# Narrow-head attentions of a two-layer decoder: the ones-times-maximum products put ahead of the transposed scores in their PSUM accumulation

## The chip, the cores and the metric

The kernel runs on one core of a Trainium2 chip. The metric is the device time of one execution in microseconds (us); before the change it is 4456.8 us, the median of three runs (4455.21 to 4457.26).

## The reference, cut to what matters

Two decoder layers over 16 sequences of 256 tokens, width 256. Three of the four attentions have 16 heads of 16 and are touched by the change: `L0_attn` (causal), `L0_xattn` (keys masked), `L1_attn` (causal, rotary positions). `L1_xattn` (heads of 64) and the two expert blocks are other code.

```python
# _L0_attn_ref / _L1_attn_ref (causal); q, k, v: [16, 16 heads, 256, 16]
s = einsum('bhqd,bhkd->bhqk', q, k) / sqrt(16); s = where(causal, s, -inf)
p = exp(s - max(s, -1)); y = einsum('bhqk,bhkd->bhqd', p, v) / sum(p)
# _L0_xattn_ref: the same without the triangle
scores = where(mask == 0, -1e9, einsum('bhqd,bhkd->bhqk', Q, K) / sqrt(16))
ctx = einsum('bhqk,bhkd->bhqd', softmax(scores), V)
```

## The kernel before, in words

`narrow_attention_phase` runs each of the three attentions as a software pipeline over the 16 sequences; one pass of the loop is a *step*. In a step TensorE (PE) does eight *groups* (`pair_of_heads`, g = 0 to 7), and behind each group two *uses* of the two bank buffers `a_ps[0]` and `a_ps[1]` (`use_bank`): M1, Y1 behind group 0; Q2B, K2B; V1, Z; Q1, K1 (behind group 3); YT0, YT1 (behind 4); YT, Q2A (behind 5); M0, OUT (behind 6); K2A, Y0 (behind 7). The uses are the projections (L1480), transposes (L1470, L1487, L1505), the transposed maxima (L1492) and the product with the values (L1500). All engines' orders are written out by hand; semaphores tie them together.

A group handles two heads of the next sequence and two of the present one:

- *s-heads*: scores with queries on partitions (L1384, `s_ps`). VectorE (DVE) takes their row maxima, negated (L1193/L1194 causal, L1196 otherwise), when `s_full` is raised.
- *t-heads*: the same scores with keys on partitions (L1388, `t_ps`), and on top of them the negated maximum of each query, added by a product of ones with `mT`, three bfloat16 pieces of the maximum (L1401 and L1402 causal, L1406 otherwise). ScalarE (ACT) takes the exponential of the sum (L1303) when `t_full` is raised.

A head of 16 is padded to 32 partitions (`lane`), so a score product uses 32 of the array's 128 rows. The four heads of a group lie in four different lanes: two lanes hold the s-heads, the other two the t-heads.
All waits of a group (for free score banks `s_taken`, `t_taken`, and for the copies of the projections and maxima) stand ahead of its first product. What DVE and ACT do between the groups matters for three uses: Q1 waits for the rounding of Z (ACT L1315, DVE L1245), YT for the division (DVE `divide`: L1254, L1257, which stands behind the maxima of group 4), and M0 for the rounding of YT. In `L1_attn`, POOL turns queries and keys (`rope`, L1100 to L1103) between Q1 and K2A.

Of the kernel before, what the change touches and what calls it, by code (L numbers as in the profile page):

```python
# [30 lines left out]
P = 128  # L31
B, S, D = 16, 256, 256
H = 16
TT = S // P
# [823 lines left out]
def narrow_attention_phase(nc, c, x_res, ident, ins, x_rest):  # L858

    n = c.name  # L860
    GROUPS, PAD = 4, 32
    ONE, DROP = c.dk, c.dk + 1
    with ExitStack() as ctx:
# [10 lines left out]
        s_ps, t_ps, a_ps = bank[0:3], bank[3:6], bank[6:8]  # L874
# [9 lines left out]
        ones3 = sb("ones3", [P, P], BF16)  # L884
# [40 lines left out]
        qT = [sb(f"qT{i}", [P, GROUPS, S]) for i in range(2)]  # L925
        kT = [sb(f"kT{i}", [P, GROUPS, S]) for i in range(2)]
# [5 lines left out]
        mT = sb("mT", [P, GROUPS, S], BF16)  # L932
# [15 lines left out]
        t_full = sem("t_full")  # L948
# [27 lines left out]
        SLOT = [0, 1, 2] * 5 + [1]  # L976
# [45 lines left out]
        with nc.Block() as block:  # L1022
# [330 lines left out]
            def _(pe):  # L1353
                def pair_of_heads(b, u, g):

                    s_of, t_of = (2 * g, 2 * g + 1) if exists(b + 1) else (), t_heads(g) if exists(b) else ()
                    if not s_of and not t_of:
                        return
                    if s_of:
                        if g == 0:  # L1360
                            pe.wait_ge(a_free[Q2A % 2], emptied(b - 1, Q2A))
                            pe.wait_ge(a_free[K2A % 2], emptied(b - 1, K2A))
                        if g == 4:
                            pe.wait_ge(a_free[Q2B % 2], emptied(b, Q2B))
                            pe.wait_ge(a_free[K2B % 2], emptied(b, K2B))
                        pe.wait_ge(s_taken, slots_free(b + 1, g))
                    if t_of:
                        if g == 0:
                            pe.wait_ge(a_free[M0 % 2], emptied(b - 1, M0))
                        if g == 4:  # L1370
                            pe.wait_ge(a_free[M1 % 2], emptied(b, M1))
                        pe.wait_ge(t_taken, slots_free(b, g))
                    pe.sem_inc(tick, 1)

                    def lane(h):
                        return slice(PAD * (h % 4), PAD * (h % 4) + PAD)

                    def tile(h, x, t):
                        return x[lane(h), h // 4, t * P:(t + 1) * P]

                    def score(h, t):
                        keys = (t + 1) * P if c.causal else S
                        to = t * (P if c.causal else S)
                        return pe.matmul(s_ps[SLOT[h]][:, to:to + keys], tile(h, qT[1 - u], t), kT[1 - u][lane(h), h // 4, 0:keys], start=t == 0, stop=t == 1 and not c.causal, skip_group_check=True)  # L1384

                    def score_turned(i, h, k):
                        q0 = k * P if c.causal else 0
                        return pe.matmul(t_ps[SLOT[2 * g + i]][:, k * S:k * S + S - q0], tile(h, kT[u], k), qT[u][lane(h), h // 4, q0:S], start=k == 0, stop=False, skip_group_check=True)  # L1388

                    for t in range(TT):  # L1390
                        for i in range(2):
                            if s_of:
                                e = score(s_of[i], t)
                                if t == 1 and not c.causal:
                                    e.then_inc(s_full, 1)
                            if t_of:
                                score_turned(i, t_of[i], t)
                    for i, h in enumerate(t_of):
                        out = t_ps[SLOT[2 * g + i]]
                        if c.causal:  # L1400
                            pe.matmul(out[:, 0:S], ones3[lane(h), :], mT[lane(h), h // 4, :], start=False, stop=False, skip_group_check=True)  # L1401
                            e = pe.matmul(out[:, S:3 * P], ones3[lane(h), :], mT[lane(h), h // 4, P:S], start=False, stop=c.held, skip_group_check=True)  # L1402
                            if c.held:
                                e.then_inc(t_full, 1)
                        else:
                            pe.matmul(out[:, :], ones3[lane(h), :], mT[lane(h), h // 4, None, :].to_broadcast([PAD, TT, S]), start=False, stop=True, skip_group_check=True).then_inc(t_full, 1)  # L1406
                    if c.causal:
                        for to, which, full in [(s_ps[SLOT[h]], tri, s_full) for h in s_of] + ([] if c.held else [(t_ps[SLOT[2 * g + i]], triT, t_full) for i, h in enumerate(t_of)]):
                            pe.matmul(to[:, 0:4 * P].rearrange("p (a k) -> p a k", k=2 * P)[:, :, 0:P], ident_bf[:, :], which[:, None, :].to_broadcast([P, TT, P]),  # L1409
                                      start=False, stop=True, skip_group_check=True).then_inc(full, 1)  # L1410
# [1167 lines left out]
```

## Time and profile before

| | |
|---|---|
| median of 3 runs | 4456.8 us |
| span of the profiled execution | 4566.7 us (its page gives no other time for it) |
| PE busy, weight loads | 3980.8 us (87%), 3216.9 us (70%) |
| VectorE, ScalarE, GpSimd busy | 58%, 43%, 50% |
| clock granted to PE | 0.921 on average |
| `L0_attn`, `L0_xattn`, `L1_attn` | about 36 to 430, 495 to 930 and 2337 to 2790 us of the span |

The profiled execution takes 110 us longer than the median run, so differences are read from its rows and set against the median. PE busy counts a matmul from its start to its modelled end, so that matmuls which follow each other overlap in it: a PE that is 99% busy may still stand for parts of a microsecond at a switch. In a timeline row `x2` means two instructions merged, and the length is that of both together.

### The profile page before, as it was taken

Reading aid. Unit: us, or ns where it says so; the run is one execution under the profiler, and the core shown is the slowest. Engines: PE = TensorE matmul, PEld = TensorE weight load, DVE = VectorE, ACT = ScalarE, POOL = GpSimd, SP = SyncE. Lnnn points to the kernel's source line nnn. Section 1 sums busy time; section 2 is a strip of 40 time slices with the busy share of each in tenths; the row PEclk is TensorE's granted clock in tenths of the full one; section 3 lists DMA queues with packets and bytes.
Section 4 is the critical chain, followed back from the end, with each engine's and each line's share of the span. In section 5 each row is a group of like instructions: output and inputs, shape, how many; then the busy total and the mean of one; then the engine's idle time right before and its main releaser. Section 6 shows DMA issues by size and latency. Waiting matters only on the chain. (4 is left out here: it accounts for less than half of the span.)

```text
span 4566.7 us, 99602 instructions
## 1 busy us (share of the span) xinstructions
PE 3980.8 (87%) x33640; PEld 3216.9 (70%) x33640; DVE 2660.8 (58%) x6267; ACT 1958.4 (43%) x4070; POOL 2261.4 (50%) x2482
## 2 busy tenths in 40 slices
PE   6999799964889999788969996999999998499991
PEld 5887577643578888677748875777677776399991
DVE  4664466568944443345546654777777766855553
ACT  2554355533222222222224443666666664155550
POOL 2332322213056666556644542766667664256665
PEclk9998799976999999899979997999999998599996
DMA  1000100001279999777710003334443441256653
GB/s 52 0 0 1 29 12 9 3 29 44 93 234 296 295 295 295 229 260 251 259 49 1 0 1 94 98 93 105 103 102 91 101 102 40 83 213 224 216 200 117
DMA packets 294489, 538.97 MB, mean 118 GB/s; under 512 B 38016, under 2 KB 136448, under 8 KB 283264
## 3 DMA queue, kind: packets, MB, share of 16 engines
q1 hardware_dynamic: 153600, 338.74, 22.3%
q0 software_dynamic: 107264, 136.38, 12.1%
q10 hardware_dynamic: 33408, 60.83, 3.5%
q8 instruction: 151, 2.47, 0.2%
q14 instruction: 66, 0.54, 0.0%
HBM read 378.53 MB, written 140.51 MB: 114 GB/s over the span
## 5 line engine op out<-in xcount | busy, mean ns | idle before, releaser
L2047 POOL DMA_INDIRECT L_ffn_xin<-zs,L_ffn_listed x464 | 501.6, 1081 | 313.6 <-issue 166.1
L562 POOL TENSOR_TENSOR L_xattn_p<-L_xattn_p,L_xattn_rsum 128x1024 f32<-128x1024 f32 x256 | 484.1, 1891 | 223.7 <-DVE L_xattn_rsum L664 219.9
L2407 POOL DMA_INDIRECT L_ffn_back<-ys,L_ffn_slots x320 | 311.6, 974 | 206.2 <-issue 88.0
L2079 PE MATMUL L_ffn_bank<-L_ffn_xT,L_ffn_w 128*128 128x256 f32 x1536 | 369.9, 384 | 9.1 <-issue 4.1
L1303 ACT ACTIVATE L_attn_pT<-L_attn_bank 128x384 f32<-128x384 f32 x512 | 223.4, 488 | 323.1 <-PE L_attn_bank L1409 177.2
L599 DVE TENSOR_REDUCE L_xattn_negmax<-L_xattn_scores 128x2 f32<-128x1024 f32 x256 | 310.5, 1213 | 82.5 <-PE L_xattn_scores L771 82.5
L698 ACT ACTIVATE L_xattn_p<-L_xattn_scores,L_xattn_negmax 128x512 f32<-128x512 f32 x512 | 346.4, 687 | 5.0 <-DVE L_xattn_negmax L599 4.3
L2146 ACT ACTIVATE L_ffn_xT<-L_ffn_bank 128x512 f32<-128x512 f32 (+1 forms) x232 | 137.8, 594 | 411.4 <-issue 182.4
L2079 PEld LDWEIGHTS L_ffn_bank<-L_ffn_xT,L_ffn_w 128*128 128x128 f32 x1536 | 278.9, 192 | 47.2 <-issue 12.1
L783 PE MATMUL L_xattn_turned<-ident,L_xattn_p 128*128 128x128 f32 x2048 | 271.2, 276 | 31.9 <-POOL L_xattn_p L562 31.9
L2298 DVE TENSOR_TENSOR L_ffn_hid<-L_ffn_sg,L_ffn_bank 128x256 f32<-128x256 f32 x192 | 80.9, 421 | 344.7 <-ACT L_ffn_sg L2154 168.5
L2052 POOL TENSOR_TENSOR L_ffn_w<-L_ffn_w,L_ffn_w 128x2048 fp32r<-128x2048 f32 x40 | 185.5, 4637 | 170.5 <-ACT L_ffn_w L2172 170.5
L1193 DVE TENSOR_REDUCE L_attn_negmax<-L_attn_bank 128x1 f32<-128x128 f32 x512 | 146.6, 286 | 211.5 <-PE L_attn_bank L1409 210.4
L783 PEld LDWEIGHTS L_xattn_turned<-ident,L_xattn_p 128*128 128x128 f32 x2048 | 231.5, 142 | 46.4 <-POOL L_xattn_p L562 40.1
L768 PE MATMUL L_xattn_scores<-L_xattn_kT,L_xattn_qT 64*128 64x512 f32 x1536 | 249.4, 430 | 14.9 <-ACT L_xattn_p L698 8.7
L1384 PE MATMUL L_attn_bank<-L_attn_kT,L_attn_qT 32*128 32x128 f32 (+1 forms) x2048 | 245.4, 356 | 13.1 <-DVE L_attn_negmax L1194 7.6
L838 PE MATMUL L_xattn_bank<-L_xattn_pT,L_xattn_v 128*64 128x256 f32 x2048 | 250.7, 387 | 1.8 <-DVE L_xattn_pT L604 0.7
L1388 PE MATMUL L_attn_bank<-L_attn_qT,L_attn_kT 32*128 32x256 f32 (+1 forms) x2048 | 246.4, 357 | 3.5 <-ACT L_attn_pT L1303 2.4
L706 ACT ACTIVATE L_xattn_pT<-L_xattn_turned 128x512 f32<-128x512 f32 x256 | 154.1, 602 | 166.4 <-PE L_xattn_turned L783 166.1
L1196 DVE TENSOR_REDUCE L_xattn_negmax<-L_xattn_bank 128x2 f32<-128x512 f32 x256 | 164.7, 686 | 85.7 <-PE L_xattn_bank L1384 84.3
L1194 DVE TENSOR_REDUCE L_attn_negmax<-L_attn_bank 128x1 f32<-128x256 f32 x512 | 212.4, 415 | 0.0
L536 POOL DMA_DIRECT2D L_xattn_mask<-in_L_xattn_mask x256 | 194.9, 762 | 22.4 <-PE L_xattn_scores L771 16.0
(385 smaller groups left out, 11427.7 us busy)
## 6 DMA issues: line engine op xcount, KB each, us to landing
L_ffn_w<-in_L_ffn_w SPq DMA_DIRECT2D x80, 1024.0 KB
L_ffn_w<-in_L_ffn_w SPq DMA_DIRECT2D x192, 384.0 KB
ys<-L_ffn_yo ACTq DMA_DIRECT2D x232, 256.0 KB
kv<-kv_v_row SPq DMA_DIRECT2D x128, 256.0 KB
L_xattn_mask<-in_L_xattn_mask POOLq DMA_DIRECT2D x256, 128.0 KB, 2.6
L_xattn_k_raw<-kv SPq DMA_DIRECT2D x128, 256.0 KB, 2.7
L_xattn_v<-kv SPq DMA_DIRECT2D x16, 2048.0 KB, 9.7
kv<-kv_k_row SPq DMA_DIRECT2D x96, 256.0 KB
```

Source lines behind the costliest of these rows:

```text
L562: pool.tensor_tensor(p[:, s % 4, :, :], p[:, s % 4, :, :], rsum[:, s % 2, :, None].to_broadcast([P, 2, c.keys]), ALU.mult).then_inc(n_read ...
L599: dve.tensor_reduce(negmax[:, s % 2, :], s_ps[s % 2][:, :, :], AX.X, ALU.max, negate=True).then_inc(m_ready, 1)
L698: e = act.activation(p[:, s % 4, i, :], s_ps[s % 2][:, i, :], ACT.Exp, bias=negmax[:, s % 2, i:i + 1], accum_out=lsum[:, s % 2, i:i + 1])
L768: pe.matmul(out[:, i, :], qT[q_piece][lane, g, t * P:(t + 1) * P], kT[k_piece][lane, g % KR, :], start=q_piece == 1, stop=False, skip_grou ...
L783: e = pe.transpose(t_ps[i][:, k * P:(k + 1) * P], p[:, s % 4, i, k * P:(k + 1) * P], ident[:, :])
L838: e = pe.matmul(to[i * c.dk:(i + 1) * c.dk, 0:S], values[:, k_, 2 * g + i, :], pT[:, g % 2, i, k_, :], start=k_ == 0, stop=k_ == c.kt - 1, ...
L1303: act.activation(pT[:, h, 0:WIDTH], t_ps[SLOT[2 * g + i]][:, 0:WIDTH], ACT.Exp, scale=c.scale).then_inc(t_taken, 1)
L1384: return pe.matmul(s_ps[SLOT[h]][:, to:to + keys], tile(h, qT[1 - u], t), kT[1 - u][lane(h), h // 4, 0:keys], start=t == 0, stop=t == 1 an ...
L1388: return pe.matmul(t_ps[SLOT[2 * g + i]][:, k * S:k * S + S - q0], tile(h, kT[u], k), qT[u][lane(h), h // 4, q0:S], start=k == 0, stop=Fal ...
L2047: pool.indirect_dma_start(xin[j % U][:, t, :], None, zs, bass.IndirectOffsetOnAxis(ap=listed[:, 2 * j + t:2 * j + t + 1], axis=0)).then_in ...
L2079: return pe.matmul(out, a[0], b[0], start=first, stop=last)
L2407: pool.indirect_dma_start(back[:, i % NG, :], None, ys, bass.IndirectOffsetOnAxis(ap=slots[:, tile, k:k + 1], axis=0)).then_inc(b_in[i % N ...
```

## The change

The ones products of the t-heads are issued at the start of the group and open the accumulation (`start=True`); the transposed scores follow and add to them. In the causal attentions the two 256-wide products come first, one for each t-head, then the two of 128. `t_full` is raised by the last transposed score of each head, where nothing follows it (`L0_attn`, `L0_xattn`).

```diff
                     def score_turned(i, h, k):
                         q0 = k * P if c.causal else 0
-                        return pe.matmul(t_ps[...][...], tile(h, kT[u], k), qT[u][lane(h), h // 4, q0:S], start=k == 0, stop=False, ...)
+                        last = k == TT - 1 and not (c.causal and not c.held)
+                        return pe.matmul(t_ps[...][...], tile(h, kT[u], k), qT[u][lane(h), h // 4, q0:S], start=False, stop=last, ...)
+                    for i, h in enumerate(t_of):
+                        out = t_ps[SLOT[2 * g + i]]
+                        if c.causal:
+                            pe.matmul(out[:, 0:S], ones3[lane(h), :], mT[lane(h), h // 4, :], start=True, stop=False, ...)
+                        else:
+                            pe.matmul(out[:, :], ones3[lane(h), :], mT[lane(h), h // 4, None, :].to_broadcast([PAD, TT, S]), start=True, ...)
+                    if c.causal:
+                        for i, h in enumerate(t_of):
+                            pe.matmul(t_ps[SLOT[2 * g + i]][:, S:3 * P], ones3[lane(h), :], mT[lane(h), h // 4, P:S], start=False, ...)
                     for t in range(TT):
                         for i in range(2):
 ...
                             if t_of:
-                                score_turned(i, t_of[i], t)
-                    for i, h in enumerate(t_of):
-                        out = t_ps[SLOT[2 * g + i]]
-                        if c.causal:
-                            pe.matmul(out[:, 0:S], ones3[...], mT[...], start=False, ...)
-                            e = pe.matmul(out[:, S:3 * P], ones3[...], mT[...], start=False, stop=c.held, ...)
-                            if c.held:
-                                e.then_inc(t_full, 1)
-                        else:
-                            pe.matmul(out[:, :], ones3[...], mT[...].to_broadcast([PAD, TT, S]), start=False, stop=True, ...).then_inc(t_full, 1)
+                                e = score_turned(i, t_of[i], t)
+                                if t == 1 and (c.held or not c.causal):
+                                    e.then_inc(t_full, 1)
```

PE in `L0_xattn`, one group with the use M0 behind it, before (semaphores keep the name of the first attention in these lists):

```order
L1384 MATMUL L_xattn_bank<-L_xattn_kT,L_xattn_qT 128x256 [waits L0_attn_s_taken,L0_attn_t_taken]
L1388 MATMUL L_xattn_bank<-L_xattn_qT,L_xattn_kT 128x256
L1384 MATMUL L_xattn_bank<-L_xattn_kT,L_xattn_qT 128x256
L1388 MATMUL L_xattn_bank<-L_xattn_qT,L_xattn_kT 128x256
L1384 MATMUL L_xattn_bank<-L_xattn_kT,L_xattn_qT 128x256
L1388 MATMUL L_xattn_bank<-L_xattn_qT,L_xattn_kT 128x256
L1384 MATMUL L_xattn_bank<-L_xattn_kT,L_xattn_qT 128x256
L1388 MATMUL L_xattn_bank<-L_xattn_qT,L_xattn_kT 128x256
L1406 MATMUL L_xattn_bank<-L_xattn_mT,L_xattn_ones 128x512 x2
L1492 MATMUL L_xattn_bank<-L_xattn_ident_bf,L_xattn_m 128x128 [waits L0_attn_a_free0,L0_attn_m_split]
```

and the same place now:

```order
L1396 MATMUL L_xattn_bank<-L_xattn_mT,L_xattn_ones 128x512 [waits L0_attn_s_taken,L0_attn_t_taken]
L1396 MATMUL L_xattn_bank<-L_xattn_mT,L_xattn_ones 128x512
L1384 MATMUL L_xattn_bank<-L_xattn_kT,L_xattn_qT 128x256
L1389 MATMUL L_xattn_bank<-L_xattn_qT,L_xattn_kT 128x256
L1384 MATMUL L_xattn_bank<-L_xattn_kT,L_xattn_qT 128x256
L1389 MATMUL L_xattn_bank<-L_xattn_qT,L_xattn_kT 128x256
L1384 MATMUL L_xattn_bank<-L_xattn_kT,L_xattn_qT 128x256
L1389 MATMUL L_xattn_bank<-L_xattn_qT,L_xattn_kT 128x256
L1384 MATMUL L_xattn_bank<-L_xattn_kT,L_xattn_qT 128x256
L1389 MATMUL L_xattn_bank<-L_xattn_qT,L_xattn_kT 128x256
L1495 MATMUL L_xattn_bank<-L_xattn_ident_bf,L_xattn_m 128x128 [waits L0_attn_a_free0,L0_attn_m_split]
```

The group's waits now stand on the first ones product; the same products run, and the last of the group is a transposed score.

PE in `L0_attn`, a group with the triangle behind it, before (bank 1 and 2 hold the s-heads, 4 and 5 the t-heads):

```order
L1384 MATMUL L0_attn_bank1<-L0_attn_kT0,L0_attn_qT0 128x128 [waits L0_attn_t_taken]
L1388 MATMUL L0_attn_bank4<-L0_attn_qT1,L0_attn_kT1 128x256
L1384 MATMUL L0_attn_bank2<-L0_attn_kT0,L0_attn_qT0 128x128
L1388 MATMUL L0_attn_bank5<-L0_attn_qT1,L0_attn_kT1 128x256
...
L1388 MATMUL L0_attn_bank5<-L0_attn_qT1,L0_attn_kT1 128x128
L1401 MATMUL L0_attn_bank4<-L0_attn_mT,L0_attn_ones3 128x256
L1402 MATMUL L0_attn_bank4<-L0_attn_mT,L0_attn_ones3 128x128
L1401 MATMUL L0_attn_bank5<-L0_attn_mT,L0_attn_ones3 128x256
L1402 MATMUL L0_attn_bank5<-L0_attn_mT,L0_attn_ones3 128x128
L1409 MATMUL L0_attn_bank1<-L0_attn_tri,L0_attn_ident_bf 128x2x128
```

and now:

```order
L1394 MATMUL L0_attn_bank4<-L0_attn_mT,L0_attn_ones3 128x256 [waits L0_attn_t_taken]
L1394 MATMUL L0_attn_bank5<-L0_attn_mT,L0_attn_ones3 128x256
L1399 MATMUL L0_attn_bank4<-L0_attn_mT,L0_attn_ones3 128x128
L1399 MATMUL L0_attn_bank5<-L0_attn_mT,L0_attn_ones3 128x128
L1384 MATMUL L0_attn_bank1<-L0_attn_kT0,L0_attn_qT0 128x128
L1389 MATMUL L0_attn_bank4<-L0_attn_qT1,L0_attn_kT1 128x256
L1384 MATMUL L0_attn_bank2<-L0_attn_kT0,L0_attn_qT0 128x128
L1389 MATMUL L0_attn_bank5<-L0_attn_qT1,L0_attn_kT1 128x256
...
L1389 MATMUL L0_attn_bank5<-L0_attn_qT1,L0_attn_kT1 128x128
L1412 MATMUL L0_attn_bank1<-L0_attn_tri,L0_attn_ident_bf 128x2x128
```

The four ones products moved from the group's end to its start, and the two t-heads alternate in them. The orders of the other engines are the same.

## Rows read from the trace of the kernel before

**Rows 1.** The page: span and number of instructions.
```profile
span 4566.7 us, 99602 instructions
```

**Rows 2.** Steps of `L0_xattn`, `L0_attn`, `L1_attn`: length, busy PE, PEld, DVE, ACT, POOL, clock, DMA.
```profile
702.00:727.32 25.32, 25.08 (x300) 18.13 (x296) 17.24 (x35) 14.46 (x28) 6.96 (x15) 1.00 0.03 10
211.70:236.00 24.30, 23.94 (x332) 19.68 (x328) 16.15 (x51) 12.32 (x26) 7.94 (x18) 1.00 0.00 0
2577.10:2603.40 26.30, 25.54 (x350) 21.08 (x346) 16.07 (x49) 12.31 (x26) 12.85 (x25) 1.00 0.00 0
```

**Rows 3.** Lines on their own: count, minimum/median/maximum in ns, first and last start.
```profile
L1406 PEld LDWEIGHTS L_xattn_bank<-L_xattn_mT,L_xattn_ones x256: 92/93/147, 523.7 to 925.1; 32*128 32x128 bf16 x128
L1384 PEld LDWEIGHTS L_xattn_bank<-L_xattn_kT,L_xattn_qT x1024: 181/185/333, 496.1 to 897.6; 32*128 32x128 f32 x171
L1401 PE MATMUL L_attn_bank<-L_attn_mT,L_attn_ones x512: 267/268/416, 65.8 to 2778.3; 32*128 32x256 bf16 x171
L1409 PE MATMUL L_attn_bank<-L_attn_tri,L_attn_ident_bf x512: 272/282/418, 40.4 to 2754.0; 128*128 128x256 bf16 x171
L1409 PE MATMUL L_attn_bank<-L_attn_triT,L_attn_ident_bf x256: 272/273/418, 2366.3 to 2778.6; 128*128 128x256 bf16 x128
```

**Rows 4.** Timeline of PE, group 4 of a step of `L0_xattn`: start, length, what.
```profile
714.67 0.48 PE L1388 MATMUL L_xattn_bank<-L_xattn_qT,L_xattn_kT 32*128 32x256 f32 x1
...
714.99 0.37 PE L1388 MATMUL L_xattn_bank<-L_xattn_qT,L_xattn_kT 32*128 32x256 f32 x1
...
715.21 0.37 PE L1388 MATMUL L_xattn_bank<-L_xattn_qT,L_xattn_kT 32*128 32x256 f32 x1
...
715.64 0.39 PE L1406 MATMUL L_xattn_bank<-L_xattn_mT,L_xattn_ones 32*128 32x512 bf16 x2
715.96 0.33 PE L1505 MATMUL L_xattn_bank<-ident,L_xattn_y_all 128*128 128x128 f32 x1
```

**Rows 5.** The same group, the weight loads.
```profile
714.78 0.18 PEld L1388 LDWEIGHTS L_xattn_bank<-L_xattn_qT,L_xattn_kT 32*128 32x128 f32 x1
...
715.96 0.20 PEld L1505 LDWEIGHTS L_xattn_bank<-ident,L_xattn_y_all 128*128 128x128 f32 x2 [0.42 <-issue]
```

**Rows 6.** Timeline of PE, end of a group of `L0_attn`.
```profile
202.79 0.28 PE L1401 MATMUL L_attn_bank<-L_attn_mT,L_attn_ones 32*128 32x256 bf16 x2
202.90 0.23 PE L1402 MATMUL L_attn_bank<-L_attn_mT,L_attn_ones 32*128 32x128 bf16 x2
```

**Rows 7.** Weight loads behind groups 3, 5 and 6 of that `L0_xattn` step.
```profile
711.63 0.30 PEld L1480 LDWEIGHTS L_xattn_bank<-L_xattn_wq,L_xattn_zT 128*128 128x128 f32 x2 [0.61 <-DVE L_xattn_zT L1245]
718.43 0.31 PEld L1470 LDWEIGHTS L_xattn_bank<-ident,L_xattn_yn 128*128 128x128 f32 x3 [0.58 <-DVE L_xattn_yn L1257]
720.81 0.23 PEld L1492 LDWEIGHTS L_xattn_bank<-L_xattn_ident_bf,L_xattn_m 128*128 128x128 bf16 x4 [0.49 <-DVE L_xattn_yT L1245]
```

**Rows 8.** Timeline of DVE behind group 4 of that step.
```profile
715.83 1.29 DVE L1196 TENSOR_REDUCE L_xattn_negmax<-L_xattn_bank 128x2 f32<-128x512 f32 x2
717.16 0.37 DVE L1254 RECIPROCAL L_xattn_rsum<-L_xattn_bank 128x16 f32<-128x16 f32 x2
```

**Rows 9.** Weight loads behind groups 3 and 5 of an `L0_attn` step.
```profile
221.03 0.53 PEld L1480 LDWEIGHTS L_attn_bank<-L_attn_wq,L_attn_zT 128*128 128x128 f32 x4 [0.34 <-DVE L_attn_zT L1245]
227.77 0.31 PEld L1470 LDWEIGHTS L_attn_bank<-ident,L_attn_yn 128*128 128x128 f32 x3 [0.31 <-issue]
```

**Rows 10.** `L1_attn`: POOL from the turn of the queries to that of the keys.
```profile
2589.42 0.87 POOL L1100 TENSOR_TENSOR L_attn_swapped<-L_attn_q_raw,L_attn_sin 128x128 f32<-128x128 f32 x2 [8.47 <-DVEq L1224]
...
2599.02 1.27 POOL L1103 TENSOR_TENSOR L_attn_kp<-L_attn_turned,L_attn_swapped 128x512 f32<-128x512 f32 x1
```

**Rows 11.** The load of K2A behind group 7 of that step.
```profile
2600.52 0.31 PEld L1487 LDWEIGHTS L_attn_bank<-ident,L_attn_kp 128*128 128x128 f32 x3 [1.03 <-issue]
```

**Rows 12.** Timeline of PE, M0 and OUT of the `L0_xattn` step (bfloat16, then float32).
```profile
720.81 0.40 PE L1492 MATMUL L_xattn_bank<-L_xattn_ident_bf,L_xattn_m 128*128 128x128 bf16 x4
721.02 0.48 PE L1480 MATMUL L_xattn_bank<-L_xattn_wo,L_xattn_yT 128*128 128x256 f32 x2
```

More of the change, by code:

```diff
@@ L1387, in score_turned @@
                         q0 = k * P if c.causal else 0
-                        return pe.matmul(t_ps[SLOT[2 * g + i]][:, k * S:k * S + S - q0], tile(h, kT[u], k), qT[u][lane(h), h // 4, q0:S], start=k == 0, stop=False, skip_group_check=True)
+                        last = k == TT - 1 and not (c.causal and not c.held)
+                        return pe.matmul(t_ps[SLOT[2 * g + i]][:, k * S:k * S + S - q0], tile(h, kT[u], k), qT[u][lane(h), h // 4, q0:S], start=False, stop=last, skip_group_check=True)
+                    for i, h in enumerate(t_of):
+                        out = t_ps[SLOT[2 * g + i]]
+                        if c.causal:
+                            pe.matmul(out[:, 0:S], ones3[lane(h), :], mT[lane(h), h // 4, :], start=True, stop=False, skip_group_check=True)
+                        else:
+                            pe.matmul(out[:, :], ones3[lane(h), :], mT[lane(h), h // 4, None, :].to_broadcast([PAD, TT, S]), start=True, stop=False, skip_group_check=True)
+                    if c.causal:
+                        for i, h in enumerate(t_of):
+                            pe.matmul(t_ps[SLOT[2 * g + i]][:, S:3 * P], ones3[lane(h), :], mT[lane(h), h // 4, P:S], start=False, stop=False, skip_group_check=True)
                     for t in range(TT):
@@ L1396, in pair_of_heads @@
                             if t_of:
-                                score_turned(i, t_of[i], t)
-                    for i, h in enumerate(t_of):
-                        out = t_ps[SLOT[2 * g + i]]
-                        if c.causal:
-                            pe.matmul(out[:, 0:S], ones3[lane(h), :], mT[lane(h), h // 4, :], start=False, stop=False, skip_group_check=True)
-                            e = pe.matmul(out[:, S:3 * P], ones3[lane(h), :], mT[lane(h), h // 4, P:S], start=False, stop=c.held, skip_group_check=True)
-                            if c.held:
-                                e.then_inc(t_full, 1)
-                        else:
-                            pe.matmul(out[:, :], ones3[lane(h), :], mT[lane(h), h // 4, None, :].to_broadcast([PAD, TT, S]), start=False, stop=True, skip_group_check=True).then_inc(t_full, 1)
+                                e = score_turned(i, t_of[i], t)
+                                if t == 1 and (c.held or not c.causal):
+                                    e.then_inc(t_full, 1)
                     if c.causal:
```

## The prediction, made before the changed kernel ran

> **What bounds the kernel now.** I read first what one step of each of the three attentions takes, then the lines on their own, then PE's timeline through single groups, and last what PE waits for between groups. PE is busy for 25.08 of the 25.32 us of a step of `L0_xattn`, 23.94 of 24.30 in `L0_attn` and 25.54 of 26.30 in `L1_attn`, at the full granted clock of 1.00, while DVE is at 17.24, 16.15 and 16.07 and ACT below 15 [rows 2]. So PE sets the step, and a part of a microsecond taken out of a group counts, unless PE stands behind that group for somebody else. The span of 4566.7 us [rows 1] is 110 us over the median; the page gives no other time of that execution. I work the change out as a difference in the span and take it off the median of 4456.8.
>
> A group is bound by its t-lanes. In `L0_xattn` the four t passes start at 714.67, 714.99, 715.21 and one spacing later, and the ones at 715.64 [rows 4], each passing 0.215 behind the one before it; the next full-height load comes at 715.96 [rows 5], 0.10 after the ones have streamed their 0.215. The s-lanes have nothing to do in that time. The first pass of a lane takes 0.32 up to the next instead of 0.215, and its row is 0.48 long against 0.37: 0.107 of float32 weight load stand bare at the head, since nothing runs that could cover them. The lane's second load starts at 714.78, when the first pass begins to stream [rows 5], so in a lane one load runs ahead, beneath the pass before it.
>
> **The change part by part.** No instruction is added or removed. Two (in `L0_xattn`) or four ones products per group go from the end to the head. There are 256/2 = 128 such groups in `L0_xattn` and 512/2 = 256 in the causal two [rows 3], 16 steps of 8 groups in each attention.
>
> *What moves off the path at the head.* The bare load is now that of the ones, in bfloat16. Its row is 93 ns against 185 ns for the float32 one [rows 3], 0.09 shorter. How much of it is bare ahead of a 32-row pass is not in the trace. Nearest is the full-height triangle: the first product behind a switch is 282 ns, those behind it 272 and 273 [rows 3], so 0.01 is bare. I take 0.01; the other end is no gain over float32, 0.107.
>
> *`L0_xattn`, t-lane.* Before: 0.107 + 4 x 0.215 + 0.215 = 1.18. Now: 0.01 + 0.215 (ones) + 4 x 0.215 = 1.085, since the float32 load of 0.107 fits beneath the ones. Gain 0.096 a group, between 0 and 0.107.
>
> *Causal, t-lane.* Before: 0.107, two passes of 0.215, two of 0.107, ones of 0.107 and 0.053. Now the first float32 load can start only when the last ones product (0.053) starts, and sticks out by 0.054. Gain 0.107 - 0.01 - 0.054 = 0.043 a group, between -0.054 and 0.107.
>
> *s-lanes.* They start two to four issues later. The two L1401, 0.268 long each [rows 3] and two issues apart, are 0.28 long together [rows 6], so two issues are 0.013. The s-lane of `L0_xattn` then ends 0.097 ahead of the t-lane, the causal one 0.12 ahead. `s_full` of `L0_xattn` comes 0.013 later from the group's start; in the causal two it hangs on the triangle and comes with the group's earlier end. `t_full` comes with the group's end, as before.
>
> *Waits.* All of a group's waits stood ahead of its first product already; now they hold the ones too, and nothing else is queued behind them that was not. What counts is where PE waits behind a group. Between a group of `L0_xattn` and a full-height load 0.42 of PEld idleness is the switch itself [rows 5]; ahead of Q1 it is 0.61, ahead of YT 0.58, ahead of M0 0.49 [rows 7], so PE stands 0.19, 0.16 and 0.07 for DVE.
>
> - Q1: DVE's rounding starts from Z, ahead of group 3. Group 3's gain becomes a longer wait: 0.
> - YT: DVE's division stands behind the maxima of group 4, which run 715.83 to 717.12, with the reciprocal at 717.16 [rows 8]. That chain hangs on `s_full` of group 4. So the gains of groups 4 and 5 are lost and the chain starts 0.013 later: -0.013.
> - M0: ACT rounds YT behind the exponentials of group 5, which come earlier by the two lost gains. The 0.07 wait goes and group 6's 0.096 counts: +0.166.
> - Groups 0, 1, 2, 7 have no wait behind them: 4 x 0.096 = 0.384.
>
> Sum 0.54 a step, x 16 = 8.6 us.
>
> *`L0_attn`.* Waits stand ahead of Q1 (0.34) and YT (0.31) [rows 9]; a load behind the triangle otherwise follows without idleness. The maxima of group 4 start with the triangle, so group 4 keeps its gain. Groups 3 and 5 lose it, six keep it: 6 x 0.043 x 16 = 4.1 us.
>
> *`L1_attn`.* POOL turns queries and keys from 2589.42 to 2600.29 [rows 10], and K2A's load follows at 2600.52 after 1.03 of idleness [rows 11]. The chain starts when DVE has taken Q1, so all between Q1 and K2A is cover: groups 4 to 7 give nothing, nor does group 3. Left are 0 to 2: 3 x 0.043 x 16 = 2.1 us.
>
> Together 8.6 + 4.1 + 2.1 = 14.8 us off the span; I forecast 4456.8 - 14.8 = 4442 us. The waits that disappear are late next nowhere else: Q1, YT and K2A stay the late ones.
>
> On the head load a page goes further. The row of 93 against 185 ns is the short load. The Trainium skill (TensorE: Matmul & The Clock Gate, Weight-path perf modes — Fast Weight Load (FWL) and DoubleRow) says that loads of 128 columns that aren't float32 go faster, measured at about twice the speed. By that the bare part would be near half of the float32 one, and the result would be rival 1's; the triangle's rows speak for less.
>
> **The rivals.**
>
> 1. *The head load is half bare, 0.053.* Then `L0_xattn` gains 0.053 a group (4 x 0.053 + 0.053 + 0.07 - 0.013 = 0.32 a step, 5.2 us) and the causal groups 0. For it: a load row cut to half. Against it: 282 against 272. 4457 - 5 = 4452 us.
> 2. *No wait eats anything*, because DVE and ACT move up wherever a group ends earlier. 128 x 0.096 + 256 x 0.043 = 23 us: 4434. Against it: Q1 and K2A hang on uses ahead of the groups.
> 3. *The lanes keep the written order.* An s pass that is written behind a t pass then starts no earlier than it. In a causal group the last s pass (0.215) starts with the last t pass of the other head (0.107 long), and the group gets longer than now: t-lanes reach that pass at 0.78, the s pass ends at 0.99 plus, against 0.93 before: +0.07 on nine groups a step, 10 us. In `L0_xattn` the group keeps its gain, but `s_full` comes 0.1 later and YT with it: 8.6 - 1.7 = 6.9. Net +3: 4460. Against it: in the causal group L1401 and L1402 are written in turn, head by head, yet both L1401 start at 202.79 and within 0.28 together, ahead of the first L1402 at 202.90 [rows 6]. That is a start out of the written order across lanes. The Trainium skill (TensorE: Matmul & The Clock Gate, Part 3: Packing small matmuls — row/col tiling) says that matmuls start and end strictly in order; the trace disagrees over this short distance, and I keep a chance for a longer one.
> 4. *Slower: going from bfloat16 to float32 within a lane empties it.* Before, a lane only went the other way. Place: behind the ones of each group. Price: a drain like the switch's 0.10 [rows 4, 5] and the float32 load bare behind it, 0.107. `L0_xattn`: 0.01 + 0.215 + 0.10 + 0.107 + 0.86 = 1.29, +0.11; causal +0.11 as well. On five and nine groups a step: 14 x 0.11 x 16 = 25 us: 4481. It decides as soon as drain and bare load together pass 0.1 in `L0_xattn`, 0.05 more than now in the causal groups. Against it: in full height OUT in float32 follows M0's four bfloat16 products at their usual 0.05 each, 720.81 to 721.02 [rows 12].
>
> That the change does not do what it says is no rival: the orders show it.
>
> **How the numbers follow.** Chances: forecast 0.53, rival 1 0.20, rival 2 0.07, rival 3 0.12, rival 4 0.08. A difference of 0.2% (9 us) is what a measurement of this kernel can tell from none. Faster by more takes the forecast and rival 2, less what an overestimate of a few hundredths of a microsecond a group would cost, plus a little of rival 1: 0.57. Rivals 1 and 3 and that rest are within 0.2%: 0.34. Slower: 0.09, rival 4 and a part of 3. The range is 4434 (rival 2) to 4461 (past rival 3), which leaves out rival 4 and the tails.
>
> **What would show it.** In the changed profile: the first ones product of a group about as long as the last was (0.38 in `L0_xattn`, not 0.48), and the group from first load to the next full-height load 1.20 instead of 1.30 in `L0_xattn`, 0.99 instead of 1.03 in the causal two. Steps of 24.8, 24.05 and 26.2 us instead of 25.3, 24.3 and 26.3. PEld's idleness at a switch without a wait becomes 2 x 0.215 + 0.10 - 0.18 = 0.35, since the last load is now that of a t pass; ahead of Q1 I expect 0.35 + 0.19 + 0.10 = 0.64, ahead of YT 0.35 + 0.16 + 0.19 + 0.01 = 0.71, ahead of M0 the bare 0.35. Wrong would be: a gap between the ones and the first t pass (rival 4); L1384's last passes starting with those of the other t-head (rival 3); a head product of 0.43 (rival 1); unchanged idleness ahead of Q1 and K2A with shorter steps (rival 2).

## The result and the profile after

The changed kernel takes 4432.4 us (median of four runs, 4430.2 to 4439.9) against 4457.0 us beside it: 24.6 us less. The ratio is 0.9941, its 95% interval 0.9930 to 0.9953, which is 21 to 31 us less. The forecast was 4442, 14.8 us less, and the lower end of its range 4434. The direction and what a group is bound by were right. The size was not, and neither was one of the three waits.

The page after (the span lies near the median this time; the 110 us by which the span of before stood over it [rows 1] were that execution's own: two later profiles of the same kernel have spans of 4462.5 and 4458.2 us):

```profile
span 4432.2 us, 99602 instructions
PE 3905.1 (88%) x33640; PEld 3199.8 (72%) x33640; DVE 2670.9 (60%) x6267; ACT 1969.4 (44%) x4070; POOL 2270.7 (51%) x2482
```

One step of `L0_xattn`, `L0_attn` and `L1_attn`, in the columns of [rows 2]:

```profile
684.75:709.41 24.66, 24.20 (x298) 18.31 (x296) 17.19 (x36) 14.46 (x28) 6.97 (x15) 1.00 0.03 11
218.00:242.01 24.01, 23.61 (x328) 19.54 (x328) 16.11 (x52) 12.34 (x28) 7.93 (x18) 1.00 0.00 0
2445.00:2471.15 26.15, 25.23 (x352) 20.89 (x348) 15.98 (x49) 12.34 (x27) 12.84 (x25) 1.00 0.00 0
```

The steps are 0.66, 0.29 and 0.15 shorter than in [rows 2]; over ten steps each the means fall from 25.317, 24.269 and 26.300 to 24.660, 24.010 and 26.148, by 0.657, 0.259 and 0.152. DVE's, ACT's and POOL's busy time did not move.

PE's timeline through group 4 of a step of `L0_xattn`, to be held against [rows 4]:

```profile
696.86 0.39 PE L1396 MATMUL L_xattn_bank<-L_xattn_mT,L_xattn_ones 32*128 32x512 bf16 x2
696.87 0.49 PE L1384 MATMUL L_xattn_bank<-L_xattn_kT,L_xattn_qT 32*128 32x256 f32 x2
697.09 0.38 PE L1389 MATMUL L_xattn_bank<-L_xattn_qT,L_xattn_kT 32*128 32x256 f32 x2
697.19 0.39 PE L1384 MATMUL L_xattn_bank<-L_xattn_kT,L_xattn_qT 32*128 32x256 f32 x2
...
697.74 0.38 PE L1389 MATMUL L_xattn_bank<-L_xattn_qT,L_xattn_kT 32*128 32x256 f32 x2
698.04 0.44 PE L1508 MATMUL L_xattn_bank<-ident,L_xattn_y_all 128*128 128x128 f32 x2
```

The two ones products last 0.39 together, the first float32 pass of the t-lanes starts 0.23 behind them and the others at their 0.215. No float32 load stands bare in these lanes; the s-lanes (0.49) still have theirs. From the group's first product to the transposes it is 1.18, where it was 1.29 in [rows 4] (714.67 to 715.96).

Weight loads, as in [rows 5] and [rows 7]: a bare switch, then ahead of Q1, YT and M0.

```profile
698.04 0.31 PEld L1508 LDWEIGHTS L_xattn_bank<-ident,L_xattn_y_all 128*128 128x128 f32 x3 [0.33 <-issue]
693.83 0.30 PEld L1483 LDWEIGHTS L_xattn_bank<-L_xattn_wq,L_xattn_zT 128*128 128x128 f32 x2 [0.63 <-DVE L_xattn_zT L1245]
700.51 0.31 PEld L1473 LDWEIGHTS L_xattn_bank<-ident,L_xattn_yn 128*128 128x128 f32 x3 [0.59 <-DVE L_xattn_yn L1257]
702.79 0.23 PEld L1495 LDWEIGHTS L_xattn_bank<-L_xattn_ident_bf,L_xattn_m 128*128 128x128 bf16 x4 [0.41 <-DVE L_xattn_yT L1245]
```

Less the switch, PE waits 0.30, 0.26 and 0.08 for DVE, where it waited 0.19, 0.16 and 0.07: one group's gain is lost ahead of Q1, one ahead of YT, none ahead of M0.

### The profile page after: what moved, and what is told of

Its sections match the earlier page's. It is cut to its first block and busy times, and to the rows that moved or that the text cites. A ratio compares the mean times of both kernels' runs of the same rounds, so it can differ in the third digit from the quotient of the medians.

```text
span 4432.2 us, 99602 instructions
## 1 busy us (share of the span) xinstructions
PE 3905.1 (88%) x33640; PEld 3199.8 (72%) x33640; DVE 2670.9 (60%) x6267; ACT 1969.4 (44%) x4070; POOL 2270.7 (51%) x2482
## 5 line engine op out<-in xcount | busy, mean ns | idle before, releaser
L2427 DVE SCALAR_TENSOR_TENSOR x_res<-L_ffn_back,L_ffn_share,x_res 128x256 f32<-128x256 f32 x320 | 152.7, 483 | 136.0 <-DMA L_ffn_back<-ys,L_ffn_slots 131.6
L1389 PE MATMUL L_attn_bank<-L_attn_qT,L_attn_kT 32*128 32x256 f32 (+1 forms) x2048 | 229.8, 343 | 0.0
```

## The experiments

Each row below is one execution: the mean of ten steps at full clock, and the *last stretch* of `L0_attn`, from about group 5 of its third last step to its end. That end is at 466.8 us of the span in the kernel before; what comes behind 430 us is the last step and the emptying of the pipeline. Ratios stand against runs of the kernel before on the same chip. Where none is given, the kernel ran once beside the others and only its trace is used. Two kernels have more than one profile: the kernel before (before, again_before, before_three) and the changed one (changed, again_after).

| kernel | `L0_attn` | `L0_xattn` | `L1_attn` | last stretch | ratio, interval |
|---|---|---|---|---|---|
| before | 24.27 | 25.32 | 26.30 | 70.5 | 1 |
| changed | 24.01 | 24.66 | 26.15 | 64.8 | 0.9941, 0.9930 to 0.9953 |
| only_xattn | 24.27 | 24.67 | 26.30 | 70.5 | 0.9970, 0.9958 to 0.9983 |
| only_causal | 24.01 | 25.32 | 26.15 | 64.9 | 0.9967, 0.9956 to 0.9979 |
| again_after | 24.01 | 24.67 | 26.15 | 64.9 | 0.9950, 0.9936 to 0.9964 |
| narrow_first | 23.74 | 24.67 | 25.98 | 64.1 | 0.9931, 0.9916 to 0.9945 |
| one_a | 24.27 | 25.20 | 26.25 | 70.4 | |
| one_b | 24.22 | 25.24 | 26.32 | 65.4 | |
| one_c | 24.28 | 25.32 | 26.31 | 65.5 | |
| again_before | 24.28 | 25.32 | 26.31 | 70.6 | |
| middle | 24.99 | 25.32 | 26.79 | 70.8 | |
| f32_head | 27.26 | 29.93 | 28.96 | 78.3 | |
| f32_tail | 28.12 | 30.03 | 29.86 | 78.5 | |
| tail_only | 24.28 | 25.31 | 26.33 | 64.0 | 0.9982, 0.9971 to 0.9993 |
| not_tail | 24.01 | 24.67 | 26.17 | 65.1 | 0.9954, 0.9935 to 0.9972 |
| at_first | 24.27 | 25.32 | 26.30 | 65.5 | |
| last_g0 | 24.27 | 25.32 | 26.32 | 70.5 | |
| last_g5 | 24.27 | 25.32 | 26.31 | 70.4 | |
| before_three | 24.27 | 25.32 | 26.30 | 70.5 | |

**Which attention, and is it repeated?** Ones ahead in `L0_xattn` alone, in the two causal attentions alone, and the changed kernel once more.

```diff
+HEAD = {'L0_attn': (), 'L0_xattn': (0, 1, 2, 3, 4, 5, 6, 7), 'L1_attn': ()}                        # only_xattn
+HEAD = {'L0_attn': (0, 1, 2, 3, 4, 5, 6, 7), 'L0_xattn': (), 'L1_attn': (0, 1, 2, 3, 4, 5, 6, 7)}   # only_causal
+ahead = g in HEAD[c.name]
```

> The ones go ahead of the scores in L0_xattn alone. Theory (the bare float32 load at a group's head is hidden, and groups 3 and 5 or 6 give it to waits): the step of L0_xattn is 24.66 us as in the changed kernel, those of L0_attn and L1_attn 24.27 and 26.30 as before; 6 x 0.108 x 16 = 10.4 us off, and up to 4 more from groups at half clock: 4444 to 4447. Rival (the gain lies mostly in the granted clock at the edges of the phases): the same steps, but a time no better than 4450.

> The ones go ahead in L0_attn and L1_attn alone. Theory: steps 24.02 and 26.15 us, L0_xattn stays at 25.32; (0.255 + 0.145) x 16 = 6.4 us off, and up to 4 more from groups at half clock: 4446 to 4451. Together with the kernel in which only L0_xattn is changed the gains add to that of the changed kernel (24 us). Rival (the phases are coupled by the clock): they don't add up within 5 us.

> The changed kernel again. Theory: steps of 24.02, 24.66 and 26.15 us to 0.02 again; the first and last steps of each phase, in which groups wait and the granted clock falls to half, differ from the first profile by some us, since code and waits there are the same. Time 4428 to 4437. Rival (edges are a fixed part of the change): the phases' lengths 433.9, 447.0 and 474.1 us come back to 0.5 us.

Medians 4448.3, 4446.8 and 4438.7 us, with 4462.6 for before on that chip: 14.3, 15.8 and 23.9 less. Each step length goes with its own attention to about 0.01 us and none with another, so the steps add: 16 x 0.65 = 10.4 us for `L0_xattn`, 16 x (0.26 + 0.15) = 6.6 us for the causal two. The whole times don't settle whether the rest adds. The two gains together are 30.1 us, 6.2 more than the 23.9 of again_after, and the expectation had given a distance over 5 to the rival. But each of these gains is uncertain by about 5 us (only_causal's interval is 9 to 20 us), so this is neither for it nor against it. By the medians `only_causal` is worth nine more than its steps, and the last stretch of `L0_attn`, 5.6 shorter, is the larger part of that. The forecast for the whole had nothing of that kind. again_after repeats the step lengths; its median is 1.7 above the range expected. The time between the first and the last transposed maxima (uses M1 and M0) of `L0_attn` is 364.2 us in the profile of the changed kernel and 360.5 in this one, so the phases' lengths don't come back to 0.5 us.

**Which products at the head?** In the causal attentions the ones over 128 queries first, those over 256 second.

```diff
-pe.matmul(out[:, 0:S], ones3[lane(h), :], mT[lane(h), h // 4, :], start=True, ...)
+pe.matmul(out[:, S:3 * P], ones3[lane(h), :], mT[lane(h), h // 4, P:S], start=True, ...)
...
-pe.matmul(out[:, S:3 * P], ones3[lane(h), :], mT[lane(h), h // 4, P:S], start=False, ...)
+pe.matmul(out[:, 0:S], ones3[lane(h), :], mT[lane(h), h // 4, :], start=False, ...)
```

> The changed kernel, but in the causal attentions the 128-wide ones product opens and the 256-wide one follows, so that 0.107 and not 0.053 of stream lies over the float32 load of the first transposed score. Theory (in a lane one load runs ahead, beneath the product before it): a causal group goes from 0.98 to 0.93 us between its first load and the triangle's; 0.05 on five groups a step of L0_attn and three of L1_attn, 8 x 0.05 x 16 = 6.7 us less than the changed kernel: 4426. Rival (loads and streams don't line up that way, the 0.05 is a cost of the change from bfloat16 to float32): groups stay at 0.98, time as the changed kernel's.

4429.4 us against 4438.7 for again_after beside it. By its steps this version beats both kernels; the intervals of the two whole times still overlap. First a causal group of the changed kernel, then one of narrow_first:

```profile
216.69 0.22 PE L1399 MATMUL L_attn_bank<-L_attn_mT,L_attn_ones 32*128 32x128 bf16 x2
216.74 0.43 PE L1389 MATMUL L_attn_bank<-L_attn_qT,L_attn_kT 32*128 32x256 f32 x2
217.01 0.38 PE L1389 MATMUL L_attn_bank<-L_attn_qT,L_attn_kT 32*128 32x256 f32 x2
...
217.54 0.28 PE L1412 MATMUL L_attn_bank<-L_attn_tri,L_attn_ident_bf 128*128 128x256 bf16 x1
```

```profile
217.16 0.27 PE L1399 MATMUL L_attn_bank<-L_attn_mT,L_attn_ones 32*128 32x256 bf16 x2
217.28 0.38 PE L1389 MATMUL L_attn_bank<-L_attn_qT,L_attn_kT 32*128 32x256 f32 x2
217.49 0.38 PE L1389 MATMUL L_attn_bank<-L_attn_qT,L_attn_kT 32*128 32x256 f32 x2
```

Behind the narrow product the first float32 pass is 0.43 long, its load sticking out by 0.054; behind the wide one it is 0.38 and nothing sticks out. The group goes from 1.050 to 0.997 us. The steps give 0.27 = 5 x 0.053 and 0.16 = 3 x 0.053, so five groups of `L0_attn` and three of `L1_attn` count, as in the change itself. Times 16 that is 6.9 us of the 9.3, and the 6.7 expected.

**Which groups count?** One group per attention and kernel.

```diff
+HEAD = {'L0_attn': (0,), 'L0_xattn': (4,), 'L1_attn': (2,)}   # one_a
+HEAD = {'L0_attn': (4,), 'L0_xattn': (5,), 'L1_attn': (4,)}   # one_b
+HEAD = {'L0_attn': (5,), 'L0_xattn': (6,), 'L1_attn': (7,)}   # one_c
+ahead = g in HEAD[c.name]
```

> The ones go ahead in one group of each phase: group 4 in L0_xattn, group 0 in L0_attn, group 2 in L1_attn. Judged by the length of a step in the profile. The prediction on record (the division behind group 4 hangs on s_full of group 4): 25.32 or more in L0_xattn. New theory (it hangs on the transposes YT1, the records of DVE overlap): 25.32 - 0.108 = 25.21. L0_attn: the record said 24.22; new theory (Y1 waits for POOL's selection behind group 7 of the step before, so group 0 is cover): 24.27. L1_attn: both 26.25.

> One group of each phase: group 5 in L0_xattn, group 4 in L0_attn, group 4 in L1_attn. L0_xattn: the record said the wait ahead of YT takes it (25.32); new theory: YT comes no earlier, but the exponentials of group 5 do, ACT's rounding of YT behind them too, and the 0.064 that PE stands ahead of M0 go: 25.25. L0_attn: group 4 is kept, 24.22. L1_attn: group 4 is cover for POOL's turn, 26.30.

> One group of each phase: group 6 in L0_xattn, group 5 in L0_attn, group 7 in L1_attn. L0_xattn: the record said kept (25.22); new theory (M0 waits for ACT and DVE, group 6 is cover): 25.32. L0_attn 24.27 and L1_attn 26.30, both covered, by either.

In `L0_xattn` group 4 alone gives 0.116, its whole gain; group 5 alone 0.073, just the wait ahead of M0; group 6 alone nothing. With 5 and 6 both moved one gain is left, if groups 0, 1, 2 and 7, which were not moved alone, keep theirs. In `L0_attn` group 0 gives 0.004, group 4 0.05, group 5 nothing; in `L1_attn` group 2 gives 0.05, groups 4 and 7 nothing. All nine came as the theory then had them, to 0.02; between profiles of kernels whose steps are alike, `L1_attn`'s differ by 0.03.

Why group 4 counts, DVE and PE show. DVE's timeline of the changed kernel, and the end of the transposes YT1 (L1508) on PE:

```profile
698.03 1.29 DVE L1196 TENSOR_REDUCE L_xattn_negmax<-L_xattn_bank 128x2 f32<-128x512 f32 x2
699.24 0.37 DVE L1254 RECIPROCAL L_xattn_rsum<-L_xattn_bank 128x16 f32<-128x16 f32 x2
```

```profile
698.65 0.49 PE L1508 MATMUL L_xattn_bank<-ident,L_xattn_y_all 128*128 128x128 f32 x3
```

The reciprocal starts at 699.24, while the maxima's row runs to 699.32: they were not what it waited for. It starts 0.10 behind the end of YT1 (698.65 + 0.49 = 699.14), and YT1 follows group 4. In the kernel before the distance is 0.11: YT1's row ends at 717.05, and the reciprocal starts at 717.16 [rows 8].

```profile
716.56 0.49 PE L1505 MATMUL L_xattn_bank<-ident,L_xattn_y_all 128*128 128x128 f32 x3
```

The chain therefore starts earlier when group 4 gets shorter, and only group 5 lies beside it.

In `L0_attn` the late one behind group 0 is POOL. PE's timeline of the kernel before, in the use Y1:

```profile
212.66 1.51 PE L1500 MATMUL L_attn_bank<-L_attn_pT,L_attn_v 128*32 128x256 f32 x32 [0.23 <-POOL L_attn_pT L1020]
```

PE waits there in some steps for the triangle that POOL zeroes. POOL's work hangs on earlier groups, so group 0's gain falls into that wait; that this is why it gives only 0.004 is read from this row, and no run tests it by itself.

**Is it the load at the head?** The ones between the two key halves; and ones and maximum in float32, at the head and at the end (the diff is cut, and its first line is in words).

```diff
+if t == 1: ones products, start=False, stop=False     # middle
-ones3 = sb("ones3", [P, P], BF16)                     # f32_head, f32_tail
+ones3 = sb("ones3", [P, P])
-mT = sb("mT", [P, GROUPS, S], BF16)
+mT = sb("mT", [P, GROUPS, S])
```

> Ones products between the passes of the first and of the second key half, in all three attentions. Theory 1 (the gain is the float32 load that no longer stands bare at a group's head): none is left, since a float32 pass opens the group again; groups of 1.36 us in L0_xattn and 1.10 in the causal attentions, steps of 25.32, 24.27 and 26.31 us as before. Theory 2 (the gain comes at the end, since a float32 pass rather than the ones stands ahead of the next full-height load): most of it stays, steps near 24.66, 24.01 and 26.15.

> Ones and the maximum's pieces in float32 instead of bfloat16 (each ones product is then two passes), at the group's head as in the changed kernel. To be read against f32_tail, which has them at the end. Theory 1 (the gain is the difference between a bare float32 load and a bfloat16 load at the head): group of L0_xattn 1.255 + 0.215 + 0.107 = 1.58 us, the same as with float32 ones at the end; causal groups 1.050 + 0.160 + 0.054 = 1.26 or a little more. Theory 2 (the gain is that ones open a lane, whatever their type): 1.47 in L0_xattn, 0.1 less than with float32 ones at the end.

> Ones and the maximum's pieces in float32, at the group's end as before. The counterpart of f32_head. Both theories: group of L0_xattn 1.363 + 0.215 = 1.58 us, causal 1.101 + 0.160 + 0.054 = 1.31 at most. Theory 1: the same length as f32_head in L0_xattn, and steps of the two within 0.1 us. Theory 2: f32_head's groups 0.1 shorter, its L0_xattn step 0.6 us shorter.

In `L0_xattn` both say theory 1. With the ones in the middle the group is 1.363 us long as before and the step 25.32. With float32 ones the place is worth 0.013 (1.992 at the head, 2.005 at the end) instead of 0.108, and the step 0.10. So in `L0_xattn` the gain is the difference in type between the loads that stand bare at the head. The absolute lengths I had wrong: a float32 product of 512 columns is two passes of 0.43, not of 0.107, four times the bfloat16 product together, and the group grew by 0.64.

In the causal attentions two results went against every theory. The first: f32_head's group is 1.578, f32_tail's 1.686. The 0.108 lies in the second t-head's lane alone. From the group's first load the first t-head ends at 1.572 in f32_head and at 1.578 in f32_tail, so for it the place is worth 0.006, as theory 1 had it; the second ends at 1.578 and 1.686. The two kernels differ in more than the place: at the head the ones of the two t-heads alternate, at the end they are written head by head. Loads of the ones in f32_tail, up to 166.07 and up to 166.1, and the four wide passes:

```profile
165.96 0.19 PEld L1401 LDWEIGHTS L_attn_bank<-L_attn_mT,L_attn_ones 32*128 32x128 f32 x1
165.96 0.30 PEld L1401 LDWEIGHTS L_attn_bank<-L_attn_mT,L_attn_ones 32*128 32x128 f32 x3
L1401 PE MATMUL L_attn_bank<-L_attn_mT,L_attn_ones x4: 374/376/471, 166.1 to 166.4; 32*128 32x256 f32 x4
```

The first t-head's load comes at 165.96, beneath the last score pass of its lane. The second's comes only at 166.07, just behind the next load of the first, although its own last score pass had started at 165.97. So it stands bare, one of the four passes is 471 ns long instead of 374 to 377, and the lane ends 0.11 late. A float32 load can thus stand bare inside a group too, where a load in another lane is written ahead of it; that the written order is the reason is read from the rows, not tested.

The second: middle's group is 1.244, not 1.10. PE in that group:

```profile
216.50 0.48 PE L1384 MATMUL L_attn_bank<-L_attn_kT,L_attn_qT 32*128 32x256 f32 x2
216.52 0.27 PE L1395 MATMUL L_attn_bank<-L_attn_mT,L_attn_ones 32*128 32x256 bf16 x1
216.61 0.23 PE L1396 MATMUL L_attn_bank<-L_attn_mT,L_attn_ones 32*128 32x128 bf16 x2
216.67 0.34 PE L1388 MATMUL L_attn_bank<-L_attn_qT,L_attn_kT 32*128 32x128 f32 x2
216.83 0.37 PE L1384 MATMUL L_attn_bank<-L_attn_kT,L_attn_qT 32*128 32x256 f32 x1
216.83 0.28 PE L1388 MATMUL L_attn_bank<-L_attn_qT,L_attn_kT 32*128 32x128 f32 x2
```

and its weight loads:

```profile
216.50 0.09 PEld L1396 LDWEIGHTS L_attn_bank<-L_attn_mT,L_attn_ones 32*128 32x128 bf16 x1
216.51 0.18 PEld L1384 LDWEIGHTS L_attn_bank<-L_attn_kT,L_attn_qT 32*128 32x128 f32 x1
```

The second s-head's load is issued at 216.51, just behind that of the narrow ones, although its lane had been free for 0.2 (its last pass starts at 216.18 and streams for 0.107); its last pass starts at 216.83, 0.87 into the group, where before it was 0.56. Something like rival 3's mechanism thus exists, here and in f32_tail, where more products stand waiting in the other lanes; the change does not reach that point.

**The phases' ends.** Ones ahead only in the last step, and everywhere but there.

```diff
+ahead = not s_of      # tail_only
+ahead = bool(s_of)    # not_tail
```

> Ones ahead only in groups without s-heads, that is in the last step of each attention. Theory 1 (the steps and the phases' ends are two separate gains, and the end of L0_attn gets its clock back from its own groups): steps as before, 24.27, 25.32 and 26.31 us; the last stretch of L0_attn (from its third last step to its end) about 65 us against 70.5, with the clock at half for about 14 us instead of 58; the whole 5 to 8 us below before. Theory 2 (that end depends on where the earlier steps have put it in time, a matter of alignment): the stretch stays 70.5 and the whole is 0 to 2 us below before.

> Ones ahead in every group that has s-heads, not in the last step. Theory 1: steps as in the changed kernel, 24.01, 24.66 and 26.15 us; the last stretch of L0_attn stays near 70.5 us at half clock; the whole about 17 us below before (0.259 + 0.657 + 0.152 a step, x 16). Theory 2: the stretch of L0_attn is 65 us as in the changed kernel, the whole about 22 us below before.

4451.8 and 4441.5 us, with 4461.9 for before: 8.0 and 20.5 less by their ratios. Steps as theory 1 had them in both. But the last stretch fell in both, to 64.0 and 65.1; each theory had it fall in one of the two only. So I moved single groups of `L0_attn` near to its end and far from it, and ran the kernel before again:

```diff
+ahead = c.name == 'L0_attn' and isinstance(b, int) and b == 0      # at_first
+ahead = c.name == 'L0_attn' and not s_of and g == 5                # last_g5
+ahead = c.name == 'L0_attn' and not s_of and g == 0                # last_g0
```

> The kernel before again, for the last step of L0_attn, in which only transposed scores are left. In the two profiles with the ones behind the scores there the granted clock stayed at half for 58 us from that step on, in the four with the ones ahead for 14 us; the time from the third last step to the phase's end was 70.5 against 64.8 us. Theory (that is part of what the change does): 70.5 and 58 us again. Rival (chance of the execution): either value.

> Ones ahead only in the first full step of L0_attn, 16 steps before its end; everything behind is as before and comes 0.25 us earlier. Theory A (the clock comes back at the end of L0_attn by how the work falls in time): the last stretch may be 65 us with the clock at half for about 14 us. Theory B (it comes back because of what changed in the last steps): 70.5 us and 58 us at half, as before.

> Ones ahead only in group 5 of the last step of L0_attn. Theory A: 70.5 or 65 us, by chance. Theory B: one group there is enough, as in the kernel that moved group 5 of every step: 65 us, clock at half for about 14 us.

> Ones ahead only in group 0 of the last step of L0_attn. Theory B: 70.5 us and 58 us at half, as in the kernel that moved group 0 of every step. Theory A: 70.5 or 65 us, by chance.

> The kernel before once more. Theory B: last stretch of L0_attn 70.5 us, clock at half for 58 us, a third time. Theory A: possibly 65 us, since the front of the attention differs from execution to execution by up to 4 us.

Stretches near the end of `L0_attn`, in the columns of [rows 2] after the length: PE, PEld, DVE, ACT, POOL, granted clock, DMA (share, GB/s). The kernel before:

```profile
428.00:432.00 4.00, 3.00 (x48) 2.34 (x50) 0.00 (x0) 1.97 (x5) 0.88 (x3) 1.00 0.00 0
440.00:444.00 4.00, 4.00 (x26) 2.90 (x26) 1.60 (x5) 1.47 (x3) 0.64 (x1) 0.50 0.00 0
448.00:452.00 4.00, 4.00 (x44) 2.14 (x40) 0.11 (x1) 0.87 (x2) 0.63 (x1) 0.50 0.02 4
484.00:488.00 4.00, 1.97 (x9) 2.00 (x10) 1.82 (x3) 0.00 (x0) 2.31 (x2) 0.50 0.21 59
```

at_first:

```profile
440.00:444.00 4.00, 4.00 (x27) 2.75 (x23) 1.08 (x3) 1.52 (x4) 0.63 (x1) 0.50 0.00 0
448.00:452.00 4.00, 2.78 (x64) 1.86 (x56) 0.00 (x0) 1.71 (x4) 0.64 (x1) 1.00 0.02 4
457.00:484.00 27.00, 7.23 (x31) 6.62 (x32) 6.79 (x18) 3.19 (x6) 15.50 (x24) 0.50 0.30 91
```

last_g5:

```profile
448.00:452.00 4.00, 4.00 (x38) 2.55 (x40) 0.69 (x1) 0.87 (x2) 0.63 (x1) 0.50 0.02 4
```

In every kernel the clock falls to half (1.2 GHz) in the last step, in which each group has two heads only and four of them follow each other without a use between; PE had been busy for 3.00 of 4 us before. In the kernel before it then stays at half to about 490. In the changed kernel and in at_first it is back after 14 us (in tail_only after 10), and the stretch is 5.7 and 5.0 us shorter. In at_first the last group of the step goes from 1.97 to 1.09 us, and the 64 products with the values behind it from 5.9 to 3.5; the groups ahead of it still run at half. The return is short, about 10 us: at 456.9 us of at_first the clock falls again and stays at half to about 484.

Theory B falls. at_first, whose changed groups lie 15 steps ahead of the fall, has the clock back; moving group 5 or 0 of the last step itself does nothing, and the kernel before never had it in three profiles. What goes with the outcome in most of the seventeen profiles with bfloat16 ones is where the fall meets the work. From the start of those four groups to the fall it is 3.07 to 3.24 us in the seven that stay at half (before, again_before, before_three, only_xattn, one_a, last_g0, last_g5), and 3.32 to 6.28 us in eight of the nine that come back (3.65 in at_first, 3.99 in the changed kernel). Two profiles don't fit. The ninth that comes back is narrow_first with 3.10, whose groups are the shortest. And middle stays at half for 55 us with the fall at 5.80. "By chance" has little for it either: the three profiles of before agree, and the two of the changed kernel; the others have one each. So the offset goes with the outcome in fifteen of seventeen; that it is the cause no run here shows, and what brings the clock back stays open.

## Why the prediction was wrong in size

| term, us | forecast | measured |
|---|---|---|
| gain of a group, `L0_xattn` / causal | 0.096 / 0.043 | 0.108 / 0.052 |
| groups kept, `L0_xattn` | 4, + 0.166 at M0, - 0.013 at YT | 6 |
| groups kept, `L0_attn`, `L1_attn` | 6, 3 | 5, 3 |
| steps x 16: `L0_xattn`, `L0_attn`, `L1_attn` | 8.6, 4.1, 2.1 | 10.5, 4.1, 2.4 |
| clock back early at the end of `L0_attn` | 0 | 5.0 (at_first) |
| the rest, shorter groups at half clock among it | 0 | 24.6 - 17.0 - 5.0 = 2.6 |

**What PE is bound by, and the head load: right.** From the first ones product to the lane's next pass it is 0.119 in a causal group for 0.107 of streaming, 0.226 for 0.213 in `L0_xattn`: 0.012 and 0.013 bare, for the 0.01 I took from the triangle's 282 against 272 [rows 3]. Rival 1, half of 0.107 bare, is out: the bfloat16 load's row is half as long as the float32 one (91 against 181 ns), its bare part a ninth. That the float32 load sticks out by 0.054 behind the narrow ones was exact.

**A group's gain: the first step that failed.** I worked it out on one t-lane and took it for both. The first t-head's lane did gain what I said: from the group's first load its last product ends 0.098 and 0.042 earlier. But a group ends with its second t-head. Before, its first product stood four issues behind the first one's and started 0.013 later; now the ones of both heads stand side by side and start 0.004 apart. That gives 0.108 and 0.052. My sum counted the issues by which the s-lanes come later and not those by which the second t-lane comes earlier. About 0.01 a group on the 14 groups a step that keep their gain is 2.2 us.

**Q1, YT, M0.** Q1 went as worked out: 0.63 of idleness for the 0.64 foreseen. At YT the step "the division stands behind the maxima of group 4, so groups 4 and 5 are lost" failed: 0.59, not 0.71. I had read the end of two merged rows and the start of the next [rows 8], 0.04 apart, as cause and effect; one group's gain was kept. M0's wait did not vanish (0.41, not 0.35): ACT's exponentials of group 5 come 0.11 earlier against YT, but so does PE, which has group 6 shortened. Together 6 x 0.108 = 0.65 a step instead of 0.54.

**The causal steps.** In `L0_attn` five groups and not six, since group 0 lies beside POOL's work; the larger gain of each made up for it: 0.259 for 0.258. That the term of 4.1 us came out is luck, two errors that cancel. In `L1_attn` exactly the three groups, POOL's turn covering the rest as [rows 10] and [rows 11] had it.

**The ends: the larger part of the error, and the step that failed most.** I multiplied steps at full clock by 16 and stopped, which put what happens at the phases' ends at nothing without a reason. Of the 9.8 us missed, 2.3 lie in the steps and 7.5 elsewhere. 5.0 of these are the clock of `L0_attn`, which came back early: so much at_first has, where no group of the last stretch is changed. At half clock a group with t-heads alone went from 1.97 to 1.89 us in the causal attentions and from 2.51 to 2.32 in `L0_xattn`; for 8 groups each in three last steps that is at most 2.8 us, of which the steps x 16 hold 1.1 already. What is then left, about 1 us, is far below the 5 us by which the 24.6 are uncertain. Without the clock the changed kernel would stand near 4438, an estimate (4432.4 + 5), still below the forecast and within its range. What the clock did is shown; why it did so is open.

**The rivals.** 2 (nothing eats the gain, 23 us) gave nearly the measured time and is wrong all the same: Q1, YT and K2A do eat it. 3 (the lanes keep the written order): the first s passes start beside the ones and out of the written order, and `s_full` comes 0.006 later, not 0.1. The Trainium skill (TensorE: Matmul & The Clock Gate, Part 3: Packing small matmuls — row/col tiling) has matmuls start strictly in order; at 696.87 and 697.09 above the second s-head's product starts 0.2 ahead of the first t-head's, which is written ahead of it. 4: there is no drain from bfloat16 to float32 within a lane (697.09 is one spacing behind 696.86).

## What to carry to other kernels

In these traces a lane that starts from empty shows its first weight load bare, 0.107 us of a float32 one and 0.012 of a bfloat16 one. So let the bfloat16 load be that one, and ahead of the next float32 load put a product long enough to cover it (the wide ones, not the narrow: 0.053 a group). Work out a group's end on the lane that ends last, both before and after, the issue offsets included. And read a releaser from what ended just before the waiting instruction on every engine, not from the row above it: a move of one group at a time tells in one run which waits eat a gain.

## What the runs showed of the hardware that I had not expected

- Products in different lanes pass each other out of the written order, but not without limit: in middle a lane stood free for 0.2 until ones in other lanes had their load, and in f32_tail a load came 0.10 after its lane could take it, just behind a load in another lane.
- Rows of DVE overlap: a reciprocal started 0.08 before the row of the reduction ahead of it ended.
- The granted clock at the end of an attention stayed at 0.50 for 58 us, or came back after 14 us for about 10 us. A difference of a few tenths of a microsecond in where it fell (3.17 us into the four groups in before, 3.65 in at_first, where one step 15 steps earlier was changed) went with the one or the other, with two exceptions in seventeen profiles. That is 5.0 us between these two, 0.11% of this kernel.
